# An attention stage on one core: where the query and key loads stand in SP's queue, and which queue carries the denominators

## The chip, the cores and the metric

The kernel runs on one core of a Trainium2 chip. The metric is the device time of one execution in microseconds (us). The engines are PE (TensorE), ACT (ScalarE), DVE (VectorE), POOL (GpSimd) and SP (SyncE, which here only issues DMAs); sixteen DMA engines move the data.

## The reference, cut to what matters

Eight batches of a 256 x 512 activation pass four layers: cross-attention, a ternary-weight feed-forward layer, a long convolution and an fp8 feed-forward layer. The change is in the first. Its attention is, with 16 heads of 16 rows each:

```python
q = einsum('oc,bct->bot', Wq, target) + bq      # 256 rows: 16 heads x 16
k = einsum('oc,bcs->bos', Wk, source) + bk
dot = einsum('bhdt,bhds->bhts', q, k) / sqrt(16)
dot = mask * dot - (1 - mask) * 1e6
amap = softmax(dot, axis=-1) * mask
x = x + tanh(g) * einsum('bhts,bhds->bhdt', amap, v)
```

## The kernel before, in words

Each layer is a phase, a block in which all engines run their own instruction lists and meet only in semaphores; the next phase begins when all engines have ended theirs. The projection phase writes the queries and keys to DRAM, split into three bf16 parts (`q_parts`, `k_parts`), as rows of 512 values (1 KB) ordered by head and then by row within the head.

The attention phase works in 16 **units**, u = 2b + h: batch b and half h of the heads (8 heads). A unit's operands are stacked in `Q` and `K`, four slots each: six blocks of 16 partitions hold products of bf16 parts, 8 further rows (partitions 96 to 103) hold mask and running maximum. `load_unit` (lines 505 to 516) fills a slot with 14 DMAs: 12 of 128 KB (16 partitions by 8 heads by 1 KB) and two of 64 KB for the mask.

Per unit, PE computes every head's scores twice. For unit u+1 (second half) and u+2 (first half) it makes the score tiles `ps_m` (L707), of which DVE takes the row maxima (L793, 32 per unit). They are turned, ACT copies them out as `mrow` (L653), and SP places them in the unit's slot (`place_max`, L529). For unit u itself PE makes the transposed scores `ps_s` (L728), ACT takes the exponential (L675), and PE multiplies by the values (L738). One extra column of the values gives the sums of the exponentials, the denominators. ACT evacuates the result in two halves, `num` and `odd_heads` (L664).

The **denominators' round trip** of a unit runs in the next unit: `gather_den` writes their rows to DRAM with two DMAs (L544, L545), waits for them, reads them back spread over 128 partitions (L547) and copies the odd heads' results beside the even ones with four DMAs (L550); DVE inverts them (L807); `store_inv` writes the inverse to DRAM (L556) and `spread_inv`, after a wait for that, reads it back broadcast to all rows (L562, 256 KB). POOL then normalises: three multiplications and additions of 128x512 (L623, L627, L631), the last into `X`. DVE takes the layer-norm statistics of unit u-2 from `X` in the third of the eight steps of unit u (L54).

POOL also makes ternary weights for the next layer in every unit (`weights`, L637 and L641, three of each, after ACT's rounding L687), from a 768 KB load `w_sweep` (L524). In every second unit it multiplies the mask by the gate (L612), and SP loads the next batch's values and mask (`load_batch`).

SP issues all DMAs from one list, in the order of the code. In unit u this is: the load of unit u+2 (after the scores of unit u-2), `gather_den` of unit u-1 with its two waits, every second time `load_batch`, `store_inv`, `place_max` of unit u+1, `spread_inv`, `load_weights` of unit u+1. PE waits for the load of unit u+2 in the middle of unit u.

Of the kernel before, what the change touches and what calls it, by code (L numbers as in the profile page):

```python
# [11 lines left out]
P = 128  # L12
B = 8
C = 256
L = 512
CT = C // P
LT = L // P
ROWT = B * CT
HEADS, HD = 16, 16
UH = 8  # L20
# [408 lines left out]
def phase_attention(core, ctx, A):  # L429
# [7 lines left out]
    DW = UH * L // P  # L437
    with ExitStack() as free:
# [14 lines left out]
        odd = sb("odd_heads", [P, 2, L], F32)  # L453
        den = sb("den", [P, 2, DW], F32)
# [38 lines left out]
        def over_batches(eng, batch):  # L493

            batch(0, 0, True, False)
            with eng.Fori(0, (B - 2) // 2) as i:
                batch(2 * i + 1, 1, False, False)
                batch(2 * i + 2, 0, False, False)
            batch(B - 1, 1, False, True)

        with nc.Block() as block:

            @block.sync
            def _(sp):
                def load_unit(b, slot, h, fresh=False):
                    for blk in range(BLOCKS):
                        for dst, src, part in ((Q, core.q_parts, Q_PART[blk]), (K, core.k_parts, K_PART[blk])):
                            s = src[bass.ds(b, 1), part, h * P:(h + 1) * P, :]
                            sp.dma_start(dst[blk * HD:(blk + 1) * HD, slot],
                                         s.rearrange("a (h d) l -> d (a h) l", d=HD)).then_inc(qk_loaded[slot], 16)  # L510
                    if fresh:
                        sp.wait_ge(zeroed[slot], 2)
                    for dst, src in ((Q, core.mask_q), (K, core.mask_k)):
                        s = src[bass.ds(b, 1)].rearrange("a r l -> r a l").to_broadcast([EXTRA, UH, L])
                        sp.dma_start(dst[MASK_ROW:MASK_ROW + EXTRA, slot], s).then_inc(qk_loaded[slot], 16)

                def load_batch(b, par):
                    sp.dma_start(V[:, par].rearrange("p a h d -> p (a h d)"),
                                 core.v_rows[bass.ds(b, 1)].rearrange("a p n -> p (a n)")).then_inc(v_loaded[par], 16)
                    sp.dma_start(mb[:, par, :], A["mask"][bass.ds(b, 1), 0, :].to_broadcast([P, L]))\  # L520
                        .then_inc(v_loaded[par], 16)

                def load_weights(u, h):
                    sp.dma_start(wc[:, h], A["w3"][bass.ds(u, 1)].rearrange("a p m l -> p (a m) l"))\  # L524
                        .then_inc(wc_loaded[h], 16)

                def place_max(v, slot, h):
                    sp.wait_ge(mrow_ready, v + 1)
                    sp.dma_start(Q[MAX_ROW:MAX_ROW + 2, slot], mrow[:]).then_inc(m_placed[h], 16)  # L529

                load_unit(0, 0, 0, fresh=True)
                load_unit(0, 1, 1, fresh=True)
                load_batch(0, 0)
                load_weights(0, 0)
                load_weights(1, 1)
                sp.wait_ge(zeroed[2], 2)
                sp.wait_ge(zeroed[3], 2)
                place_max(0, 0, 0)

                def gather_den(u, h, b):  # L540

                    sp.wait_ge(u_ready, 2 * u + 2)
                    rows = core.den_rows[h].rearrange("(g two) l -> two g l", two=2)
                    sp.dma_start(rows[0], num[HD:P:32, h, :]).then_inc(den_out[h], 16)  # L544
                    sp.dma_start(rows[1], odd[HD:P:32, h, :]).then_inc(den_out[h], 16)  # L545
                    sp.wait_ge(den_out[h], 32 * (b + 1))
                    sp.dma_start(den[:, h, :], core.den_rows[h].rearrange("q (s n) -> (q s) n", n=DW))\  # L547
                        .then_inc(den_placed[h], 16)
                    for g in range(4):
                        sp.dma_start(num[32 * g + HD:32 * g + 32, h, :], odd[32 * g:32 * g + HD, h, :])\  # L550
                            .then_inc(num_placed[h], 16)

                def store_inv(u, h):

                    sp.wait_ge(inv_ready, u + 1)
                    sp.dma_start(core.inv_rows[h].rearrange("q (s n) -> (q s) n", n=DW), inv[:, h, :])\  # L556
                        .then_inc(inv_out[h], 16)

                def spread_inv(h, b):

                    sp.wait_ge(inv_out[h], 16 * (b + 1))
                    sp.dma_start(inv_all[:, h, :], core.inv_rows[h].unsqueeze(1).to_broadcast([UH, HD, L]))\  # L562
                        .then_inc(all_placed[h], 16)

                def batch(b, par, first, last):
                    for h in range(2):
                        u = 2 * b + h
                        if not last:
                            if not first:
                                sp.wait_ge(scores_done, 2 * STEPS * (u - 1))  # L570
                            load_unit(b + 1, 2 * (1 - par) + h, h)
                        if not (first and h == 0):
                            gather_den(u - 1, 1 - h, b + h - 1)
                        if h == 1 and not last:
                            if not first:
                                sp.wait_ge(pv_step, 2 * STEPS * b)
                                sp.wait_ge(w_ready, 2 * b)
                            load_batch(b + 1, 1 - par)
                        if not (first and h == 0):
                            store_inv(u - 1, 1 - h)  # L580
                        if h == 0:
                            place_max(u + 1, 2 * par + 1, 1)
                        elif not last:
                            place_max(u + 1, 2 * (1 - par), 0)
                        if not (first and h == 0):
                            spread_inv(1 - h, b + h - 1)
                        if not (first and h == 0) and not (last and h):
                            sp.wait_ge(w_ternary, 3 * u)
                            load_weights(u + 1, 1 - h)
                    if last:  # L590
                        gather_den(u, h, b)
                        store_inv(u, h)
                        spread_inv(h, b)

                over_batches(sp, batch)

            @block.gpsimd
            def _(pool):
                for slot in (1, 3):
                    nc.gpsimd.memset(Q[96:P, slot], 0.0).then_inc(zeroed[slot], 1)  # L600
                    nc.gpsimd.memset(K[96:P, slot], 0.0).then_inc(zeroed[slot], 1)
# [3 lines left out]
                def batch(b, par, first, last):  # L605
                    for h in range(2):
                        u = 2 * b + h
                        if not (first and h == 0):
                            normalise(u - 1, 1 - h, 1 - par if h == 0 else par, b + h - 1)
                        if h == 0:  # L610
                            pool.wait_ge(v_loaded[par], batch_loads(b, par))
                            nc.gpsimd.tensor_tensor(mb[:, par, :], mb[:, par, :],  # L612
                                                    core.tanh_g[:, 0:1].to_broadcast([P, L]), ALU.mult)\
                                .then_inc(gate_ready, 1)
                            pool.wait_ge(gate_ready, b + 1)
                        weights(u, h)
                    if last:
                        normalise(u, h, par, b)

                def normalise(u, h, par, b):  # L620

                    pool.wait_ge(all_placed[h], 16 * (b + 1))
                    nc.gpsimd.tensor_tensor(inv_all[:, h, :], inv_all[:, h, :], mb[:, par, :], ALU.mult)\  # L623
                        .then_inc(w_ready, 1)
                    pool.wait_ge(w_ready, u + 1)
                    pool.wait_ge(num_placed[h], 64 * (b + 1))
                    nc.gpsimd.tensor_tensor(num[:, h, :], num[:, h, :], inv_all[:, h, :], ALU.mult)\  # L627
                        .then_inc(att_ready, 1)
                    pool.wait_ge(att_ready, u + 1)
                    xt = X[:, u:u + 1, :]  # L630
                    nc.gpsimd.tensor_tensor(xt, xt, num[:, h:h + 1, :], ALU.add).then_inc(x_updated, 1)  # L631
# [1197 lines left out]
```

## Time and profile before

| | |
|---|---|
| median of 3 runs | 1381.76 us (1378.74 to 1382.11) |
| the profiled execution | 1371.15 us, span of its instructions 1369.3 us |
| PE, DVE busy | 1113.3 us (81%), 1033.2 us (75%) |
| ACT, POOL busy | 668.1 us (49%), 523.4 us (38%) |
| row maxima L793, DVE | 512 instructions, 683 ns each, 322.2 us |
| exponentials L675, ACT | 256 instructions, 1022 ns each, 249.9 us |
| q_stack and k_stack loads | 96 each of 128 KB, from SP |

A row of the profile gives a group's busy time and, behind the bar, how long the engine had stood idle just before those instructions and who released it. The timeline gives, for each instruction or merged run of them, its start, duration, line and tiles. A DMA row's duration is the time that the issuing queue spent on it, not the transfer. All times in the rows are counted from the span's start.

### The profile page before, as it was taken

To read this page: it belongs to the slowest core of one execution; us is meant where nothing else is said; L and a number is where in the kernel's file an instruction comes from. 1 tells how busy PE (TensorE), PEld (TensorE's weight loads), DVE (VectorE), ACT (ScalarE), POOL (GpSimd) and SP (SyncE) were. 2 spreads that over 40 slices of the span, in tenths; PEclk is the share of its full clock that TensorE was granted. 3 is DMA by queue.
4 is the path that set the end of the run, shared out by engine and by line. 5 is a ranking of instruction groups with operands and counts; after the bars stand their busy time and mean duration, and the time that the engine had idled before them with its cause. 6 is when DMAs were issued, how large, how long until landed. Compare 5 with 4: busy or idle time off the path is not lost. (4 is left out here: it accounts for less than half of the span.)

```text
span 1369.3 us, 16346 instructions
## 1 busy us (share of the span) xinstructions
PE 1113.3 (81%) x4725; PEld 447.5 (33%) x4802; DVE 1033.2 (75%) x1587; ACT 668.1 (49%) x783; POOL 523.4 (38%) x384
## 2 busy tenths in 40 slices
PE   0887279998879987983799998599999999259777
PEld 0443112222222222220344444344444444134232
DVE  5765488887767877751799997388788887767898
ACT  0355308776657766684466665211000000386796
POOL 0466601244332442355011111477888787000021
PEclk9999659999989999997999999799999999579889
DMA  7398797677756776621311110111111111000011
GB/s 266 127 338 319 199 146 83 119 153 108 125 90 124 151 111 115 114 71 58 151 47 46 40 36 16 35 62 62 62 62 50 58 62 46 1 0 0 0 62 62
DMA packets 84274, 129.33 MB, mean 94 GB/s; under 512 B 13544, under 2 KB 53864, under 8 KB 83696
## 3 DMA queue, kind: packets, MB, share of 16 engines
q1 hardware_dynamic: 84224, 128.72, 38.8%
q8 instruction: 24, 0.39, 0.1%
q14 instruction: 26, 0.21, 0.1%
HBM read 104.44 MB, written 21.89 MB: 92 GB/s over the span
## 5 line engine op out<-in xcount | busy, mean ns | idle before, releaser
L793 DVE TENSOR_REDUCE mneg<-ps_m 128x1 f32<-128x512 f32 x512 | 322.2, 683 | 93.8 <-PE ps_m L707 78.3
L1337 PE MATMUL ps_y<-kv,toeplitz_sb 128*128 128x512 f32 x640 | 279.6, 596 | 8.7 <-POOL kv L1249 8.7
L675 ACT ACTIVATE probs<-ps_s 128x1024 f32<-128x1024 f32 x256 | 249.9, 1022 | 51.9 <-PE ps_s L728 51.9
L707 PE MATMUL ps_m<-k_stack,q_stack 128*128 128x512 bf16 x489 | 181.9, 410 | 55.3 <-DMA k_stack<-mask_k 50.4
L1337 PEld LDWEIGHTS ps_y<-kv,toeplitz_sb 128*128 128x128 f32 x640 | 121.1, 191 | 155.0 <-issue 155.0
L728 PE MATMUL ps_s<-q_stack,k_stack 128*128 128x512 bf16 x492 | 151.0, 387 | 21.1 <-ACT probs L675 11.2
L738 PE MATMUL ps_o<-probs,v_all 128*17 128x512 f32 x1024 | 140.1, 620 | 0.4 <-ACT probs L675 0.4
L1249 POOL TENSOR_TENSOR kv<-vT,ctxT_sb 128x2048 f32<-128x2048 f32 x32 | 118.7, 3711 | 40.0 <-PE ps_y L1337 32.6
L972 PE MATMUL ps_g<-w,xT_f 128*128 128x512 bf16 x491 | 116.7, 384 | 8.4 <-DVE h_f L1119 6.6
L623 POOL TENSOR_TENSOR inv_all<-inv_all,mb_b 128x512 f32<-128x512 f32 x16 | 20.4, 1274 | 254.9 <-DMA inv_all<-inv_rows 254.9
L707 PEld LDWEIGHTS ps_m<-k_stack,q_stack 128*128 128x128 bf16 x512 | 42.2, 99 | 219.4 <-DVE mneg L793 104.5
L1403 DVE TENSOR_TENSOR z<-ps_y,ctxT_sb 128x1024 f32<-128x1024 f32 x64 | 77.9, 1218 | 47.3 <-PE ps_y L1337 47.3
L1302 ACT ACTIVATE w_anchor<-w_f 128x512 f32<-128x512 f32 x32 | 20.1, 628 | 180.6 <-DMA w_f<-in_w 180.6
L1154 POOL TENSOR_TENSOR X<-X,down_sums 128x512 f32 (+1 forms) x16 | 20.5, 1283 | 195.6 <-ACT down_sums L1015 195.6
L1660 PE MATMUL ps_fp<-w 128*128 128x512 bf16 x251 | 67.7, 423 | 21.5 <-DVE w L1727 10.9
L1411 DVE TENSOR_REDUCE vT<-z 128x256 f32<-128x2304 f32 x32 | 81.7, 2553 | 1.1
L54 DVE BATCH_NORM_STATS2 bn<-X (+1 forms) x64 | 42.3, 682 | 42.8 <-POOL X L631 21.2
L728 PEld LDWEIGHTS ps_s<-q_stack,k_stack 128*128 128x128 bf16 x512 | 45.8, 98 | 81.0 <-ACT probs L675 33.9
L641 POOL TENSOR_SCALAR w<-w_sweep 128x512 bf16<-128x512 f32 x48 | 70.4, 1488 | 1.3
L1027 ACT ACTIVATE sg_f<-ps_g,sc_f 128x512 f32<-128x512 f32 x64 | 42.7, 686 | 57.0 <-PE ps_g L972 37.7
L972 PEld LDWEIGHTS ps_g<-w,xT_f 128*128 128x128 bf16 x512 | 48.4, 99 | 65.1 <-DVE h_f L1119 10.3
L326 PE MATMUL ps_a<-xn_a,w_qkv 128*128 128x512 f32 x64 | 30.6, 622 | 38.4 <-DVE xn_a L365 38.4
(163 smaller groups left out, 1662.6 us busy)
## 6 DMA issues: line engine op xcount, KB each, us to landing
w_sweep<-in_w SPq DMA_DIRECT2D x8, 1536.0 KB, 8.5
q_stack<-q_parts SPq DMA_DIRECT2D x96, 128.0 KB
k_stack<-k_parts SPq DMA_DIRECT2D x96, 128.0 KB
w_sweep<-in_w SPq DMA_DIRECT2D x16, 768.0 KB, 6.5
w_sweep<-in_w SPq DMA_DIRECT2D x16, 512.0 KB, 3.3
toeplitz_sb<-in_toeplitz SPq DMA_DIRECT2D x32, 256.0 KB, 2.6
w_f<-in_w SPq DMA_DIRECT2D x32, 256.0 KB, 2.9
q_parts<-qk_part SPq DMA_DIRECT2D x24, 256.0 KB, 4.0
```

The lines of the kernel that those rows point to most:

```text
L641: nc.gpsimd.tensor_scalar(core.w3[:, m].rearrange("p a b -> p (a b)")[:, u * L:(u + 1) * L], wc[:, h, m, :], MAGIC, None, ALU.subtract).th ...
L675: nc.scalar.activation(pr[:, k % 2, 2 * slot:2 * slot + 2, :], S[:, 2 * slot:2 * slot + 2, :], ACT.Exp).then_inc(exp_done, 1)
L707: nc.tensor.matmul(M[:, bank(j), :], Q[:, slot, hd, tc * P:(tc + 1) * P], K[:, slot, hd, :], start=True, stop=True).then_inc(max_mm, 1)
L728: mm = nc.tensor.matmul(S[:, g, :], K[:, slot4, hd, (k % LT) * P:(k % LT + 1) * P], Q[:, slot4, hd, :], start=True, stop=True)
L738: mm = nc.tensor.matmul(O[32 * g:32 * g + HD + 1, :], V[:, par, sc, h * UH + 2 * g + G, :], pr[:, k % 2, g, :], start=(sc == 0), stop=(sc ...
L793: nc.vector.tensor_reduce(mneg[:, h, tile % LT, tile // LT:tile // LT + 1], M[:, bank(j), :], AX.X, ALU.max, negate=True).then_inc(max_red, 1)
L972: mm = nc.tensor.matmul(G[:, c % 2, j, :], xT[:, par, k, :], wt[:, k, c * L:(c + 1) * L], start=(k == 0), stop=(k == LT - 1))
L1249: nc.gpsimd.tensor_tensor(kv[:, g % 2].rearrange("p l (b j i) -> p (l b) j i", b=B, j=GROUP), over_j(group(vT, g)), over_i(group(cT, g)), ...
L1337: mm = nc.tensor.matmul(Y[:, q % 3, l2, :], T[:, g % 2, (lt - m) * P:(lt - m + 1) * P], kv[:, g % 2, m, :], start=(m == 0), stop=(m == lt))
L1403: nc.vector.tensor_tensor(z[:, g % 2, NB // 2 * half:NB // 2 * (half + 1), :, 0:GROUP], Y[:, q % 3].rearrange("p l (b j i) -> p (l b) j i" ...
L1411: nc.vector.tensor_reduce(group(vT, g), z[:, g % 2], AX.X, ALU.add).then_inc(red_ready, 1)
L1660: mm = nc.tensor.matmul(D[:, r, :], h8[:, j % 4, L * t + r * P:L * t + (r + 1) * P], proj[:, ot, :], start=(i == 0 and t == 0), stop=(i == ...
```

## The change

- `load_unit` reads rows of `q_parts` and `k_parts` that are ordered by row within the head first, then by head, so that one partition's eight heads are 8 KB in a row. The projection weights and biases are permuted on the host (`by_dim`) so that the rows are produced in that order. Number and size of the DMAs stay.
- In SP's list the load of unit 2 stands before the first `place_max`, and in unit u the load of unit u+3 is the last entry, after `load_weights`, with a wait for the scores of unit u-1.
- `gather_den`, `store_inv` and `spread_inv` leave SP and are issued by POOL: `gather_den` of unit u-1 ahead of the gate and the ternary weights of unit u, the other two and the normalisation after them. Before, the normalisation stood ahead of the weights.
- SP's list is written out for all batches instead of looping.

```diff
-                                         s.rearrange("a (h d) l -> d (a h) l", d=HD)).then_inc(qk_loaded[slot], 16)
+                                         s.rearrange("a (d h) l -> d (a h) l", d=HD)).then_inc(qk_loaded[slot], 16)
...
                 load_weights(0, 0)
+                load_unit(1, 2, 0, fresh=True)
                 load_weights(1, 1)
-                sp.wait_ge(zeroed[2], 2)
-                sp.wait_ge(zeroed[3], 2)
                 place_max(0, 0, 0)
...
                     for h in range(2):
                         u = 2 * b + h
-                        if not last:
-                            if not first:
-                                sp.wait_ge(scores_done, 2 * STEPS * (u - 1))
-                            load_unit(b + 1, 2 * (1 - par) + h, h)
-                        if not (first and h == 0):
-                            gather_den(u - 1, 1 - h, b + h - 1)
                         if h == 1 and not last:
                             if not first:
                                 sp.wait_ge(pv_step, 2 * STEPS * b)
                                 sp.wait_ge(w_ready, 2 * b)
                             load_batch(b + 1, 1 - par)
-                        if not (first and h == 0):
-                            store_inv(u - 1, 1 - h)
                         if h == 0:
                             place_max(u + 1, 2 * par + 1, 1)
                         elif not last:
                             place_max(u + 1, 2 * (1 - par), 0)
-                        if not (first and h == 0):
-                            spread_inv(1 - h, b + h - 1)
                         if not (first and h == 0) and not (last and h):
                             sp.wait_ge(w_ternary, 3 * u)
                             load_weights(u + 1, 1 - h)
-                    if last:
-                        gather_den(u, h, b)
-                        store_inv(u, h)
-                        spread_inv(h, b)
-
-                over_batches(sp, batch)
+                        if u + 3 < 2 * B:
+                            if u:
+                                sp.wait_ge(scores_done, 2 * STEPS * u)
+                            load_unit((u + 3) // 2, (u + 3) % 4, (u + 3) % 2, fresh=u == 0)
+                for b in range(B):
+                    batch(b, b % 2, b == 0, b == B - 1)
...
             def _(pool):
+                def gather_den(u, h, b):
+                    pool.wait_ge(u_ready, 2 * u + 2)
+                    rows = core.den_rows[h].rearrange("(g two) l -> two g l", two=2)
+                    pool.dma_start(rows[0], num[HD:P:32, h, :]).then_inc(den_out[h], 16)
+                    pool.dma_start(rows[1], odd[HD:P:32, h, :]).then_inc(den_out[h], 16)
+                    pool.wait_ge(den_out[h], 32 * (b + 1))
+                    pool.dma_start(den[:, h, :], core.den_rows[h].rearrange("q (s n) -> (q s) n", n=DW))\
+                        .then_inc(den_placed[h], 16)
+                    for g in range(4):
+                        pool.dma_start(num[32 * g + HD:32 * g + 32, h, :], odd[32 * g:32 * g + HD, h, :])\
+                            .then_inc(num_placed[h], 16)
+                def store_inv(u, h):
+                    pool.wait_ge(inv_ready, u + 1)
+                    pool.dma_start(core.inv_rows[h].rearrange("q (s n) -> (q s) n", n=DW), inv[:, h, :])\
+                        .then_inc(inv_out[h], 16)
+                def spread_inv(h, b):
+                    pool.wait_ge(inv_out[h], 16 * (b + 1))
+                    pool.dma_start(inv_all[:, h, :], core.inv_rows[h].unsqueeze(1).to_broadcast([UH, HD, L]))\
+                        .then_inc(all_placed[h], 16)
...
                         if not (first and h == 0):
-                            normalise(u - 1, 1 - h, 1 - par if h == 0 else par, b + h - 1)
+                            gather_den(u - 1, 1 - h, b + h - 1)
...
                         weights(u, h)
+                        if not (first and h == 0):
+                            store_inv(u - 1, 1 - h)
+                            spread_inv(1 - h, b + h - 1)
+                            normalise(u - 1, 1 - h, 1 - par if h == 0 else par, b + h - 1)
                     if last:
+                        gather_den(u, h, b)
+                        store_inv(u, h)
+                        spread_inv(h, b)
                         normalise(u, h, par, b)
...
+    def by_dim(v):
+        return np.ascontiguousarray(v.reshape(v.shape[:-1] + (CT, P // HD, HD)).swapaxes(-1, -2).reshape(v.shape))
```

## Rows read from the trace of the kernel before

**Rows 1.** Windows: busy PE, PEld, DVE, ACT, POOL; granted clock, DMA share, GB/s.

```profile
205.00:646.00 441.00, 372.54 (x2019) 102.16 (x2058) 312.30 (x529) 304.27 (x351) 167.77 (x151) 0.95 0.62 108
```

**Rows 2.** Waits between 160 and 650 us: total us, times, longest.

```profile
POOL inv_all L623 <- DMA inv_all<-inv_rows: 254.9, 16, 28.8
...
PE ps_m L707 <- DMA k_stack<-mask_k: 50.4, 11, 22.2
```

**Rows 3.** Timeline of ACT: start, us, line, tiles, count, idle and releaser.

```profile
220.98 0.57 ACT L653 ACTIVATE mrow<-ps_m 16x512 bf16<-16x512 bf16 x1
...
244.89 0.57 ACT L653 ACTIVATE mrow<-ps_m 16x512 bf16<-16x512 bf16 x1
...
254.42 0.60 ACT L664 ACTIVATE odd_heads<-ps_o 128x512 f32<-128x512 f32 x1 [0.85 <-PE ps_o L738]
...
326.54 0.57 ACT L653 ACTIVATE mrow<-ps_m 16x512 bf16<-16x512 bf16 x1
...
603.13 0.57 ACT L653 ACTIVATE mrow<-ps_m 16x512 bf16<-16x512 bf16 x1
```

**Rows 4.** Timeline of DVE: the statistics of the second unit.

```profile
262.18 0.68 DVE L54 BATCH_NORM_STATS2 bn<-X  x1
```

**Rows 5.** Timeline of SP's queue: one unit, from mrow to mrow.

```profile
296.45 0.70 SPq L529 DMA_DIRECT2D q_stack<-mrow  x1
...
300.07 0.67 SPq L562 DMA_DIRECT2D inv_all<-inv_rows  x1
...
301.65 0.33 SPq L509 DMA_DIRECT2D q_stack<-q_parts  x1
...
309.27 0.50 SPq L545 DMA_DIRECT2D den_rows<-odd_heads  x1
...
320.06 0.36 SPq L547 DMA_DIRECT2D den<-den_rows  x1
...
327.13 0.70 SPq L529 DMA_DIRECT2D q_stack<-mrow  x1
```

**Rows 6.** Timeline of PE: the stall of that unit.

```profile
319.82 0.60 PE L707 MATMUL ps_m<-k_stack,q_stack 128*128 128x512 bf16 x1 [4.41 <-DMA k_stack<-mask_k]
```

**Rows 7.** Windows: unit loads, weight sweep, stores of the stage before; columns as above.

```profile
183.00:184.00 1.00, 1.00 (x2) 0.15 (x2) 1.00 (x2) 0.00 (x0) 0.00 (x0) 0.50 1.11 114
...
193.00:194.00 1.00, 1.00 (x3) 0.20 (x2) 1.00 (x3) 0.00 (x0) 0.18 (x1) 0.50 1.00 414
...
154.00:156.00 2.00, 0.17 (x1) 0.09 (x1) 0.51 (x3) 0.00 (x0) 0.00 (x0) 0.50 1.03 343
```

**Rows 8.** Timeline of SP's queue with empty DMA queues, at the end.

```profile
633.14 2.44 SPq L550 DMA_DIRECT2D num<-odd_heads  x4
...
635.63 0.58 SPq L556 DMA_DIRECT2D inv_rows<-inv  x1
...
637.31 0.64 SPq L562 DMA_DIRECT2D inv_all<-inv_rows  x1
```

**Rows 9.** Timeline of POOL at the end of the stage.

```profile
612.22 1.04 POOL L612 TENSOR_TENSOR mb_b<-mb_b,tanh_g 128x512 f32<-128x512 f32 x1
...
613.35 2.00 POOL L637 TENSOR_SCALAR w_sweep<-w_sweep 128x512 f32<-128x512 f32 x3
...
615.43 4.40 POOL L641 TENSOR_SCALAR w<-w_sweep 128x512 bf16<-128x512 f32 x3
...
641.11 1.26 POOL L623 TENSOR_TENSOR inv_all<-inv_all,mb_b 128x512 f32<-128x512 f32 x1 [7.32 <-DMA inv_all<-inv_rows]
...
643.79 1.26 POOL L631 TENSOR_TENSOR X<-X,num 128x512 f32<-128x512 f32 x1
```

**Rows 10.** Timeline of PE: its first work and its first scores.

```profile
176.38 1.60 PE L707 MATMUL ps_m<-k_stack,q_stack 128*128 128x512 bf16 x3 [22.20 <-DMA k_stack<-mask_k]
...
204.75 0.59 PE L728 MATMUL ps_s<-q_stack,k_stack 128*128 128x512 bf16 x2
```

**Rows 11.** Timeline of SP's queue: the first placement of the maxima.

```profile
199.14 0.81 SPq L529 DMA_DIRECT2D q_stack<-mrow  x1
```

More of the change, by code:

```diff
@@ L534, in _ @@
                 load_weights(0, 0)
+                load_unit(1, 2, 0, fresh=True)
                 load_weights(1, 1)
-                sp.wait_ge(zeroed[2], 2)
-                sp.wait_ge(zeroed[3], 2)
                 place_max(0, 0, 0)
[L540 to L563, printed above, removed]
                 def batch(b, par, first, last):
@@ L1810 @@
         "x": arr("x"), "ctx": arr("ctx_2048"), "mask": arr("mask_Bx1x2048_fk1"), "g_xattn": arr("g_xattn"),
-        "g_ffn": arr("g_ffn"), "bq": columns(inputs["L0_xattn_bq"]), "bk": columns(inputs["L0_xattn_bk"]),
+        "g_ffn": arr("g_ffn"), "bq": columns(by_dim(inputs["L0_xattn_bq"])), "bk": columns(by_dim(inputs["L0_xattn_bk"])),
         "mask_cols": np.ascontiguousarray(inputs["mask_Bx1x2048_fk1"].reshape(B, LT, P).transpose(2, 0, 1)),
         "bv": arr("L0_xattn_bv"),
-        "wqT": np.ascontiguousarray(inputs["L0_xattn_Wq"].T), "wkT": np.ascontiguousarray(inputs["L0_xattn_Wk"].T),
+        "wqT": by_dim(inputs["L0_xattn_Wq"].T), "wkT": by_dim(inputs["L0_xattn_Wk"].T),
         "wvT": np.ascontiguousarray(inputs["L0_xattn_Wv"].T),
```

## The prediction

> **What bounds the kernel now.** Of the views I read the one by stretch first: the attention stage is 441 us of the 1369 us span, and only its code changes. In it DVE is busy 312 us, PE 373, ACT 304, POOL 168, and the DMA engines 0.62 of the time [rows 1]. No engine is full, so what matters is what each unit waits for. The timeline of ACT gives the length of a unit, as `mrow` (L653) comes once in each. From the second to the third it is 23.9 us. From the second to the sixteenth it is 603.13 - 220.98 = 382.1 us in 14 units, 27.3 us each [rows 3]. The 23.9 us are the floor that PE and DVE allow when nothing is late; 14 x 3.4 = 48 us of the stage are waits above it.
>
> The view of waits names them: PE waits 50.4 us for the loads of Q and K [rows 2]. (POOL's 254.9 us in the same view cost nothing as long as no one waits for POOL.) The timeline of SP's queue shows why the load is late. After `mrow` SP places it at 296.45, but issues `spread_inv` only at 300.07 and the unit's load from 301.65 on; the two `den_rows` DMAs, issued behind that load at 308.7 and 309.27, have landed only when the next entry goes out at 320.06, 10.8 us later, since they queue behind 1.7 MB [rows 5]. PE starts the first tile on this load at 319.82, after 4.41 us of waiting [rows 6], 18.2 us after the load's first issue. Next `mrow`: 30.7 us after the last one [rows 5].
>
> **The change, part by part.**
>
> *Position of the loads.* "Three units ahead" is a new index, not a new place. Before, the load of unit u+3 is the first entry of SP's unit u+1; now it is the last of unit u, with the same wait for the scores of unit u-1. In both cases `place_max` of unit u+1 and `load_weights` stand directly ahead. What is gone from between is `spread_inv`: between 0.9 us (its issue and a gap) and the 3.6 us of the unit above [rows 5]. The load then starts about 2 us after `mrow`, and its 18.2 us fit the unit to within some tenths. I put a unit that waits for nothing else at 24.2 us, against the floor of 23.9: that would save 14 x 3.1 = 43 us.
>
> *The longer pieces.* Eight rows of 1 KB become one of 8 KB. What that is worth depends on what holds the loads at 114 GB/s with the DMA engines full, where the 6 KB pieces of `w_sweep` go at 414 [rows 7]. It is not the 1 KB piece by itself: the stores of the projection stage, also in 1 KB pieces but over 128 partitions, go at 343 [rows 7]. A load writes only 16 partitions, before and after. So I take it as unchanged, 1.2 us per 128 KB; the other end of the bound is 343 to 414 GB/s, 5 us per unit instead of 16. The Trainium skill, SBUF — State Buffer, "Door 1: The DMA port swizzle", gives the reason: 16 neighbouring partitions reach 4 of 16 ports, which by the page's 435 GB/s is 109 GB/s. By that rule the trace agrees, and nothing is gained from longer pieces.
>
> *The start.* PE begins at 176.38 on the first load and reaches the first scores at 204.75 [rows 10], soon after `place_max` of unit 0 is issued at 199.14 into an empty queue [rows 11]. Now the load of unit 2 and a sweep stand ahead of it. The sweeps end at about 197 (414 GB/s until 194 [rows 7]); without the second of them the load of unit 2 begins at 195. 12 x 1.2 + 2.4 (two masks of 8 partitions, reckoned at half that rate) = 17 us, and 2 for the sweep: the placement lands at 216 instead of before 204.75. **+11 us** at the unchanged rate; 0 if loads ran at 343.
>
> *The round trip on POOL.* Off SP, `den_rows` no longer queue behind the load. But POOL waits for each landing itself, in line with its own work. The engine had 168 of 441 us of work [rows 1]; now everything between is serial. From rows with empty DMA queues, per unit: first `den_rows` issue 0.6 and the trip of the second 1.7 (`inv_rows` at 635.63 had landed by 637.31); `den` and four `num` 0.35 + 2.44 = 2.8; half of a gate 0.5; weights 613.35 to 619.83, 6.5; `inv_rows` 1.7; `inv_all` 637.31 to 641.11, 3.8; normalising 641.11 to 645.05, 3.9 [rows 8, 9]. Sum **21.5 us**. Two prices are missing.
>
> First, POOL's own issue of a DMA, which this trace doesn't show. Bounds: 0 more than on SP, whose nine cost 5.0 us [rows 5, 8], and 1 us each, +4 (POOL's shortest instruction, a clip, takes 0.67 [rows 9]). I take 0.25 each, +2.3. The Trainium skill, DMA: Bandwidth & Descriptors, "Latency and other measured facts", has 1 us to the first byte on this path against 0.6 on SP's; three trips would add 1.2 us, inside these bounds.
>
> Second, sharing the DMA engines with the load, which is in flight 18 us of each unit, from 4 us after `mrow`. That is when `inv_rows` and `inv_all` go. In SP's single queue `inv_all` went ahead of the load; now both run at once. An engine's 8 KB share of one 128 KB DMA takes 1.2 us, so each turn taken with a load costs 1.2. Least: 0. Most: the 10.8 us of `den_rows` behind a whole load [rows 5]. `inv_rows` is one turn, 1.2; `inv_all` has 256 KB of 2 KB pieces, at least a few turns: I take 2.5, 3.0 us. Sum +4.2; it is nearer the low end, as turns are taken, not a whole load waited out. The skill page's "Queues, rings and completion order" says that an engine goes round its queues packet by packet; no row here shows two data queues at once.
>
> POOL's cycle: 21.5 + 2.3 + 4.2 = **28.0 us**, above 24.2. So POOL is the bound. It makes the others late as soon as it lags 7.2 us: DVE's statistics of unit u-2 run 7.2 us after `odd_heads` is evacuated (255.02 to 262.18 [rows 3, 4]), they wait for POOL's last addition, and behind them on DVE stand the maxima for which PE waits.
>
> *The sum*, along POOL. Its first gather starts at 231 + 11 = 242. 12 cycles with a load in flight, 12 x 28.0 = 336; 3 without (units 13 to 15), 3 x 23.8 = 71; last round trip without weights 21.5 - 6.5 - 0.5 + 2.3 = 17. End 666, against 645.05 before [rows 9]: **+21 us**. 1371.15 + 21 = 1392 for the profiled execution; that lies 10.6 us below the median of the runs, which gives 1403. The weights' move ahead of the normalisation costs nothing more: ACT's rounding is done before POOL, being late, arrives. SP's written-out list issues the same DMAs; I cost it at nothing, since SP waits for `mrow` anyway.
>
> **The rivals.**
>
> *POOL keeps up* (the other side). If POOL's cycle is at most 24.2 us, sharing and issue costing under 2.7 us together, units run at 24.2: 43 saved, less 11 at the start, and about 6 at the end, where units 14 and 15 are shorter than POOL's cycle. -26: 1356. For it: it needs only quick turns, and the weights can overlap ACT. Against: three trips that POOL waits out and 11 us of arithmetic in 24 us leave no slack, and any lag pushes the next trips into the next load. The decisive point is 24.2; the break-even with before is lower in rate, 26.2 us per cycle, (645 - 242 - 71 - 17)/12.
>
> *The longer pieces do speed the loads.* Then they take 5 us, nothing is contended, the start is 11 us earlier (17.4 us from issue to first tile becomes 7) and no +11. -35 -11 = -46: 1336. For it: no row shows 1 KB pieces loaded into 128 partitions. Against: the stores at 343.
>
> *Gain and loss cancel*: sharing at 2.4 us per unit, 1378 to 1386.
>
> *The turns are dearer*: 4 us more per cycle is 12 x 4 = 48: 1451.
>
> **Numbers.** POOL the bound and slower 0.47, cancelling 0.08, POOL keeps up 0.31, faster loads 0.14. Within 0.3% (4 us) of before a measurement can't tell it from no change. Faster 0.45, same 0.08, slower 0.47. The likeliest is 1403; its own range is 1387 to 1451. Since cases of both signs hold much, the range reaches down to the faster loads: 1336 to 1450.
>
> **What would show it.** Right: `mrow` to `mrow` 27 to 29 us and steady; POOL without idle time except on landings; DVE's statistics waiting for POOL's addition; PE waiting for DVE, no longer for loads; `inv_all` taking over 6 us from issue to L623; first scores at about 216. Wrong: units of 24 us; unit loads above 200 GB/s; POOL's DMAs landing in 2 us beside a load; first scores at 205.

## The result, and the profile after

The changed kernel takes 1479.68 us (median of 4 runs, 1478.55 to 1481.6) against 1381.22 us before. The ratio is 1.0717, interval 1.0699 to 1.0736. The profiled execution takes 1478.55 us, its span is 1476.8 us, against 1371.15 us before. The change costs 107 us there.

The attention stage first, by the view of stretches, with the columns of [rows 1]:

```profile
205.00:750.00 545.00, 391.52 (x2060) 106.44 (x2060) 312.09 (x527) 304.16 (x351) 246.01 (x295) 0.85 0.51 88
```

545 us in place of 441 [rows 1], with the same work on DVE (312) and ACT (304). POOL has 78 us more, its own DMA issues. The DMA engines are less busy than before (0.51 against 0.62), so the stage lacks neither work done nor bandwidth: it waits. The view of waits of the attention stage (total, times, longest) says for what:

```profile
PEld ps_m L703 <- DVE mneg L789: 206.0, 160, 10.3
ACT probs L671 <- PE ps_s L724: 177.0, 96, 19.5
DVE bn L54 <- POOL X L627: 127.1, 14, 15.4
POOL inv_all L585 <- DMA inv_rows<-inv: 117.3, 16, 11.8
POOL inv_all L619 <- DMA inv_all<-inv_rows: 104.0, 16, 9.6
POOL den L570 <- DMA den_rows<-odd_heads: 29.5, 15, 9.9
```

It is read from the bottom up. POOL waits 117.3 + 104.0 us for the two trips of the inverses; DVE's statistics wait 127.1 us for POOL's last addition, 14 times; PE waits for DVE's maxima and ACT for PE. PE's wait for unit loads [rows 2] is gone but for the first one. One whole cycle of POOL, nearly the same in every unit but the first, by its timeline (start, duration, line, tiles, and in brackets the idle time ahead and who ended it):

```profile
492.43 0.60 POOL L567 DMA_DIRECT2D den_rows<-num  x1
493.04 0.57 POOL L568 DMA_DIRECT2D den_rows<-odd_heads  x1
494.99 0.58 POOL L570 DMA_DIRECT2D den<-den_rows  x1 [1.39 <-DMA den_rows<-odd_heads]
495.56 1.95 POOL L573 DMA_DIRECT2D num<-odd_heads  x4
497.52 1.05 POOL L601 TENSOR_TENSOR mb_b<-mb_b,tanh_g 128x512 f32<-128x512 f32 x1
498.67 2.00 POOL L633 TENSOR_SCALAR w_sweep<-w_sweep 128x512 f32<-128x512 f32 x3
500.75 4.40 POOL L637 TENSOR_SCALAR w<-w_sweep 128x512 bf16<-128x512 f32 x3
505.11 0.65 POOL L579 DMA_DIRECT2D inv_rows<-inv  x1
515.56 0.64 POOL L585 DMA_DIRECT2D inv_all<-inv_rows  x1 [9.81 <-DMA inv_rows<-inv]
523.76 1.26 POOL L619 TENSOR_TENSOR inv_all<-inv_all,mb_b 128x512 f32<-128x512 f32 x1 [7.56 <-DMA inv_all<-inv_rows]
...
526.44 1.26 POOL L627 TENSOR_TENSOR X<-X,num 128x512 f32<-128x512 f32 x1
527.65 0.60 POOL L567 DMA_DIRECT2D den_rows<-num  x1
```

The cycle is 35.2 us. Half of it, 18.65 us, lies between the issue of `inv_rows` at 505.11 and the first multiplication at 523.76, where the same two trips take 637.31 - 635.63 and 641.11 - 637.31, 5.5 us, on empty queues [rows 8, 9]. The other trip, `den_rows`, is awaited at 493 to 495, when no load is in flight: 1.95 us. On DVE and in SP's queue, same unit:

```profile
527.88 0.69 DVE L54 BATCH_NORM_STATS2 bn<-X  x1 [9.05 <-POOL X L627]
```

```profile
501.92 0.64 SPq L529 DMA_DIRECT2D q_stack<-mrow  x1
502.61 0.41 SPq L524 DMA_DIRECT2D w_sweep<-in_w  x1
503.07 0.43 SPq L509 DMA_DIRECT2D q_stack<-q_parts  x1
...
509.00 0.31 SPq L515 DMA_DIRECT2D k_stack<-mask_k  x1
```

The load begins at 503.07, two microseconds ahead of `inv_rows`, and at 18 us for a load [rows 5, 6] it has landed at about 521; by stretches of one microsecond the bytes stop at 522. The first trip runs within it and has landed 6 us before that, at 515.56; the second ends with it. The sweep of 768 KB issued at 502.61 is in flight too, until about 507.

### The profile page after: what moved, and what is told of

It is laid out like the page before. It is cut to its first block and busy times, and to the rows that moved or that the text cites. A ratio compares the mean times of both kernels' runs of the same rounds, so it can differ in the third digit from the quotient of the medians.

```text
span 1476.8 us, 16091 instructions
## 1 busy us (share of the span) xinstructions
PE 1131.9 (77%) x4802; PEld 449.3 (30%) x4802; DVE 1033.9 (70%) x1587; ACT 668.0 (45%) x783; POOL 601.8 (41%) x528
## 5 line engine op out<-in xcount | busy, mean ns | idle before, releaser
L703 PE MATMUL ps_m<-k_stack,q_stack 128*128 128x512 bf16 x512 | 196.0, 420 | 125.6 <-DVE mneg L789 103.2
L724 PE MATMUL ps_s<-q_stack,k_stack 128*128 128x512 bf16 x512 | 164.6, 407 | 25.3 <-DMA q_stack<-mrow 13.9
L54 DVE BATCH_NORM_STATS2 bn<-X (+1 forms) x64 | 42.4, 684 | 148.7 <-POOL X L627 127.1
L968 PE MATMUL ps_g<-w,xT_f 128*128 128x512 bf16 x512 | 120.0, 383 | 7.1 <-DVE h_f L1115 6.3
L1656 PE MATMUL ps_fp<-w 128*128 128x512 bf16 x256 | 66.6, 414 | 22.5 <-DVE w L1723 12.3
L619 POOL TENSOR_TENSOR inv_all<-inv_all,mb_b 128x512 f32<-128x512 f32 x16 | 20.2, 1263 | 104.0 <-DMA inv_all<-inv_rows 104.0
L955 PE MATMUL ps_d<-w,hT_f 128*128 128x512 bf16 x256 | 59.5, 387 | 1.6 <-ACT hT_f L996 1.6
```

Of the source, the lines that this page charges most:

```text
L703: nc.tensor.matmul(M[:, bank(j), :], Q[:, slot, hd, tc * P:(tc + 1) * P], K[:, slot, hd, :], start=True, stop=True).then_inc(max_mm, 1)
L724: mm = nc.tensor.matmul(S[:, g, :], K[:, slot4, hd, (k % LT) * P:(k % LT + 1) * P], Q[:, slot4, hd, :], start=True, stop=True)
L968: mm = nc.tensor.matmul(G[:, c % 2, j, :], xT[:, par, k, :], wt[:, k, c * L:(c + 1) * L], start=(k == 0), stop=(k == LT - 1))
L1656: mm = nc.tensor.matmul(D[:, r, :], h8[:, j % 4, L * t + r * P:L * t + (r + 1) * P], proj[:, ot, :], start=(i == 0 and t == 0), stop=(i == ...
```

## The experiments

The theory after the first profile: the two trips of the inverses are slow only because a load is in flight that is bound by the ports through which it writes its few neighbouring partitions, and POOL adds them up in line with its own work. Rivals: the 8 KB pieces make each turn at a DMA engine long; DMAs from POOL are slow in themselves; the gathering and its waits on POOL are what costs; the loss lies in the start.

**Piece size.** `after_1k`: the changed kernel with the layout of before, pieces of 1 KB.

```diff
-   s.rearrange("a (d h) l -> d (a h) l", d=HD)).then_inc(qk_loaded[slot], 16)
+   s.rearrange("a (h d) l -> d (a h) l", d=HD)).then_inc(qk_loaded[slot], 16)
```

> The changed kernel with the 1 KB pieces of before (rows ordered by head again); everything else as changed. Theory of the pieces: each of POOL's small pieces waits for one piece of the unit load on its DMA engine, 1.2 us at 8 KB and 0.15 at 1 KB. Then the trip of inv_rows falls from about 9.8 us to about 3, inv_all from 8.2 to under 5, POOL's cycle from 34 to about 25 us, and the time to about 1370 us. Theory of the ports: POOL's pieces wait for the full write ports, whatever the piece; trips and time stay, about 1479 us.

Measured: 1473.9 us, ratio 1.0715 (1.0669 to 1.076). The same two trips in it:

```profile
502.83 0.65 POOL L579 DMA_DIRECT2D inv_rows<-inv  x1
512.48 0.63 POOL L585 DMA_DIRECT2D inv_all<-inv_rows  x1 [9.00 <-DMA inv_rows<-inv]
520.49 1.26 POOL L619 TENSOR_TENSOR inv_all<-inv_all,mb_b 128x512 f32<-128x512 f32 x1 [7.37 <-DMA inv_all<-inv_rows]
```

9.65 and 8.0 us, against 10.45 and 8.2. Pieces an eighth as long shorten the trips by 0.8 and 0.2 us at most, where the theory of the pieces asked for 3 and under 5 us: that rival falls. The prediction priced a turn by a DMA's 8 KB share of an engine; that share is the same in both layouts, so this run does not test that price. The 10.45 us of the trip themselves refute it.

`before_8k`: the kernel before, with the 8 KB pieces alone.

> The kernel before with the 8 KB pieces alone. If the four write ports that 16 partitions reach hold the load, nothing moves: loads at about 110 GB/s, 1381 us within 5. If the piece's length held it, a load would take under 8 us instead of 16, and the time would fall to about 1335 us.

Measured: 1381.5 us, ratio 1.003 (1.001 to 1.005). First tile on a load at 179.09 us, in place of 176.38 [rows 10]. The longer piece gives nothing, by the interval it is a hair slower.

**The ports.** `before_spread`: the kernel before, each block of 16 rows in every sixth partition of 96 instead of 16 neighbours. `Q` and `K` are permuted alike, so the sums over partitions are the same.

```diff
-   sp.dma_start(dst[blk * HD:(blk + 1) * HD, slot],
+   sp.dma_start(dst[blk:BLOCKS * HD:BLOCKS, slot],
```

> The kernel before, same DMAs, bytes and 1 KB pieces; only the 16 partitions of a block are taken in steps of 6 (blk, blk+6, ... blk+90) instead of side by side. Theory of the ports: the load goes at over 200 GB/s and takes under 9 us instead of 16, PE's waits for loads go, units fall to 24 us and the first tile starts 7 us earlier: 1320 to 1335 us. If the pieces or the source hold the load: 1381 us.

Measured: **1318.12 us, ratio 0.9581 (0.9548 to 0.9614)**. One microsecond within a load, by stretch (columns as in [rows 1]), and `mrow` of two units:

```profile
393.00:394.00 1.00, 1.00 (x9) 0.13 (x8) 1.00 (x2) 0.36 (x1) 1.00 (x1) 1.00 1.11 211
```

```profile
456.32 0.57 ACT L653 ACTIVATE mrow<-ps_m 16x512 bf16<-16x512 bf16 x1
480.21 0.57 ACT L653 ACTIVATE mrow<-ps_m 16x512 bf16<-16x512 bf16 x1
```

The DMA engines are as full as before, but move 211 GB/s instead of 114 [rows 7]. Every unit from the second on now takes 23.9 us: the floor that the prediction read from [rows 3], and no wait for loads is left but for the first one.

`before_spread_8k` adds the 8 KB pieces to it.

> The kernel before with the spread partitions and the 8 KB pieces together. In the run with 1 KB pieces the load went at about 205 GB/s and the units at 23.9 us, their floor. If the pieces now hold the load, the first tile starts up to 3 us earlier and the time falls to 1314; if the ports still hold it (13 of 16 reached, three twice), 1318 as with 1 KB.

Measured: 1319.1 us, ratio 0.9612 (0.9585 to 0.9638). Piece length is worth nothing at this rate either. But at this rate something else comes near: SP needs longer to issue a load that is spread. Its queue and the mean of 8 us within the first load of `before_spread`:

```profile
163.02 0.60 SPq L509 DMA_DIRECT2D q_stack<-q_parts  x1
163.66 0.60 SPq L509 DMA_DIRECT2D k_stack<-k_parts  x1
```

```profile
162.00:170.00 8.00, 0.00 (x0) 0.00 (x0) 6.33 (x5) 0.00 (x0) 8.00 (x3) 0.50 0.64 201
```

One DMA of 128 KB goes out every 0.64 us (0.47 in the kernel before), which is 205 GB/s; the load runs at 201, with the DMA engines busy for only 0.64 of the time. The first load of the spread kernels is thus held by SP's issuing, and says nothing of what the ports or longer pieces could give beyond that. In the later units a sweep ahead of the load builds up a backlog, and there the 211 GB/s stand at full engines.

`before_step2` interleaves only pairs of blocks, each in every second partition of 32.

```diff
-   sp.dma_start(dst[blk * HD:(blk + 1) * HD, slot],
+   sp.dma_start(dst[blk // 2 * 32 + blk % 2:(blk // 2 + 1) * 32:2, slot],
```

> The kernel before with blocks 2k and 2k+1 interleaved, each block in every second partition of 32, instead of every sixth of 96. Theory of the partition range (what counts is over how wide a range of partitions one DMA writes): 32 neighbouring partitions give twice the 110 GB/s of 16, so 0.6 us per 128 KB, a load of 8 us, units of 23.9 us and a time like that of steps of six, ratio 0.957 to 0.962. Rival (what helps is only a range of near 96 partitions, or that two DMAs behind each other write into different places): 110 to 160 GB/s, loads of 11 to 16 us, ratio 0.965 to 1.00.

Measured: 1317.82 us, ratio 0.9559 (0.9479 to 0.964; only 2 runs, hence the wide interval). Within a load:

```profile
393.00:394.00 1.00, 1.00 (x7) 0.31 (x4) 0.67 (x2) 0.51 (x2) 0.92 (x2) 1.00 1.11 202
```

Sixteen partitions spread over a range of 32 are enough for about 205 GB/s, nearly twice the rate of 16 neighbours. The Trainium skill, SBUF — State Buffer, "Door 1: The DMA port swizzle", has it so: 32 neighbouring partitions reach 8 of 16 ports, 16 reach 4. By that rule the traces agree in the ratio, at 202 to 211 and 114 GB/s; the 109 GB/s for 16 partitions that the prediction took from the page is exceeded here, by the 114, and over 14 us of the first loads of the kernel before by a mean of 122.

**The start.** `after_first`: the changed kernel with `place_max(0, 0, 0)` and the second sweep back ahead of the load of unit 2.

```diff
-                load_unit(1, 2, 0, fresh=True)
                 load_weights(1, 1)
                 place_max(0, 0, 0)
+                load_unit(1, 2, 0, fresh=True)
```

> The changed kernel with the first placement of the maxima and the second weight sweep issued ahead of the load of unit 2. Theory: the first scores start at about 205 us instead of 218, and the time falls by 13 us to 1466. If the load of unit 2 is then late for the middle of unit 0, less than that: 1475.

Measured: 1463.94 us, ratio 1.0642 (1.058 to 1.0704), 2 runs that lie 10 us apart. First scores at 206.79 in place of 217.92, and by the two traces the stage's last statistics on DVE run 9.7 us earlier. `before_first` is the mirror: the kernel before with this start alone.

```diff
+                load_unit(1, 2, 0, fresh=True)
                 load_weights(1, 1)
...
+                            if not (first and h == 0):
                                 load_unit(b + 1, 2 * (1 - par) + h, h)
```

> The kernel before with the start of the change alone: the load of unit 2 stands ahead of the second sweep and of the first placement, all else as before. My theory (position only, as in the prediction, and as the 13 to 15 us of the run with the placement put back ahead): first scores at 217 to 218 instead of 205, everything behind it shifted, 11 to 13 us slower: about 1385 here against 1372 to 1376, ratio 1.008 to 1.010. Rival (the unit load that is out of the way early is won back in units 1 and 2, which then wait for no load): ratio 1.000 to 1.003.

Measured: 1389.01 us, ratio 1.0079 (1.0041 to 1.0116), 11.1 us above the kernel before as it ran beside it (1377.91). First scores:

```profile
219.90 1.03 PE L730 MATMUL ps_s<-q_stack,k_stack 128*128 128x512 bf16 x2 [13.37 <-DMA q_stack<-mrow]
```

The start costs 11 us alone and about 10 within the change.

**What stretches the trips.** `after_spread`: the changed kernel with steps of six, so that a load is in flight half as long.

> The changed kernel, only with each block's 16 partitions taken in steps of 6, as in the run of the kernel before with that edit. If POOL's trips are slow because the loads keep four write ports full (theory of the ports), the loads end after 8 us, inv_rows and inv_all fall from 9.8 and 8.2 us to about 3 and 5, POOL's cycle from 34 to 24 or 26 us, the first scores start at about 205: 1325 to 1355 us. If the trips are slow because any second queue beside a load is served late, they stay near 9 and 8 us until the load ends, which is at half the time: about 1400.

Measured: 1375.02 us, ratio 1.0019 (0.9998 to 1.0039), above what was expected. POOL's rows:

```profile
424.00 0.60 POOL L567 DMA_DIRECT2D den_rows<-num  x1
...
436.66 0.65 POOL L579 DMA_DIRECT2D inv_rows<-inv  x1
442.52 0.63 POOL L585 DMA_DIRECT2D inv_all<-inv_rows  x1 [5.21 <-DMA inv_rows<-inv]
447.16 1.27 POOL L619 TENSOR_TENSOR inv_all<-inv_all,mb_b 128x512 f32<-128x512 f32 x1 [4.00 <-DMA inv_all<-inv_rows]
...
451.06 0.60 POOL L567 DMA_DIRECT2D den_rows<-num  x1
```

The trips take 5.9 and 4.6 us, about half of before, yet the cycle is 27.1 us: 16.6 of POOL's work, issues and first trip (to 436.66, and from 447.16 on) and 10.5 of the inverses' trips. That is over the 23.9 us that the others need, so POOL stays the bound. My expectation had put the two trips at 3 and 5 us, 8 together, and the time at 1325 to 1355 us; its rival, trips near 9 and 8 us and about 1400, is missed too. So this run shows that a shorter load shortens the trips, not that the ports as such are what holds them.

`after_few_bytes`: from unit 4 on each load carries one of the eight heads (the other operands stay those of earlier units, so this part of the computation is not that of the reference). The number of DMAs and their places are the same.

```diff
+                    hs = UH if fresh else 1
-   sp.dma_start(dst[blk * HD:(blk + 1) * HD, slot],
-                s.rearrange("a (d h) l -> d (a h) l", d=HD)).then_inc(qk_loaded[slot], 16)
+   sp.dma_start(dst[blk * HD:(blk + 1) * HD, slot, 0:hs],
+                s.rearrange("a (d h) l -> d (a h) l", d=HD)[:, 0:hs]).then_inc(qk_loaded[slot], 16)
```

> The changed kernel, but from unit 4 on the loads of Q and K carry one head of eight (16 KB instead of 128 KB in each of the 12 DMAs); the rest of the slot keeps older data. Number of DMAs, semaphores and order stay. Every theory that blames the load's bytes in flight: inv_rows about 2 us, inv_all about 4, POOL's cycle 22 to 24.5 us, ended by the units of 24 us, 1340 to 1355 us with the 13 us of the start still lost. If POOL's issuing or its order is the cause: cycle stays at 34 us, 1470.

Measured: 1356.65 us, ratio 0.9886 (0.9854 to 0.9918).

```profile
437.29 0.65 POOL L580 DMA_DIRECT2D inv_rows<-inv  x1
440.24 0.63 POOL L586 DMA_DIRECT2D inv_all<-inv_rows  x1 [2.31 <-DMA inv_rows<-inv]
444.70 1.27 POOL L620 TENSOR_TENSOR inv_all<-inv_all,mb_b 128x512 f32<-128x512 f32 x1 [3.83 <-DMA inv_all<-inv_rows]
```

Trips of 3.0 and 4.5 us, a cycle of 24 us, and units of 23.9. With the bytes gone and all DMAs and waits still there, the loss is gone: it is the load in flight, not POOL's issuing, that stretches the trips. The changed kernel's own last units, which have no load to make, say the same. First `inv_rows` and `inv_all` beside a sweep alone, then with nothing beside them:

```profile
675.59 0.64 POOL L579 DMA_DIRECT2D inv_rows<-inv  x1
678.58 0.64 POOL L585 DMA_DIRECT2D inv_all<-inv_rows  x1 [2.36 <-DMA inv_rows<-inv]
...
739.10 0.57 POOL L579 DMA_DIRECT2D inv_rows<-inv  x1
741.11 0.63 POOL L585 DMA_DIRECT2D inv_all<-inv_rows  x1 [1.43 <-DMA inv_rows<-inv]
```

`inv_rows` takes 2.0 us alone, so DMAs from POOL are not slow in themselves, and 3.0 beside the sweep, the same as here: about 1 us of the stretched trip is the sweep's, which the prediction left out, and some 7.5 us the load's.

**Whose trip is it?** `after_act_store`: the changed kernel with `store_inv` issued from ACT's queue after `mrow`, so that the trip begins without POOL. The line removed is one of POOL's list, the ones added are ACT's.

```diff
-                            store_inv(u - 1, 1 - h)
...
+                    act.wait_ge(inv_ready, u + 1)
+                    act.dma_start(core.inv_rows[h].rearrange("q (s n) -> (q s) n", n=DW), inv[:, h, :])\
+                        .then_inc(inv_out[h], 16)
```

> The changed kernel, but inv_rows is issued from ACT's queue, after the copy of mrow, instead of from POOL's. It then goes out 2 us ahead of the load instead of some us behind its start. Theory: the trip is slow only because the load is in flight; ahead of it it takes 2 us from any queue, POOL's cycle falls by about 8 us to 26, about 1385 us. If it still takes over 6 us, then a second hardware queue is served late as well, behind the load issued after it.

Measured: 1449.77 us, ratio 1.0564 (1.053 to 1.060), far above what was expected.

```profile
424.93 0.72 POOL L579 DMA_DIRECT2D inv_all<-inv_rows  x1
440.90 1.26 POOL L611 TENSOR_TENSOR inv_all<-inv_all,mb_b 128x512 f32<-128x512 f32 x1 [15.25 <-DMA inv_all<-inv_rows]
```

The store is issued at 420.30, two microseconds ahead of the load (422.47), and POOL has no wait for it; but `inv_all` alone takes 16.0 us instead of 8.2. The wait has moved from one trip to the other; of 18.65 us only 2.7 are saved.

`after_half`: the start put right, and both DMAs of the inverses back in SP's list ahead of the unit's load. Only the gathering, the weights and the normalisation stay on POOL. The lines added are SP's, the ones removed POOL's.

```diff
+                        if u:
+                            store_inv(u - 1, 1 - h)
                         if h == 0:
                             place_max(u + 1, 2 * par + 1, 1)
                         elif not last:
                             place_max(u + 1, 2 * (1 - par), 0)
+                        if u:
+                            spread_inv(1 - h, b + h - 1)
...
-                            store_inv(u - 1, 1 - h)
-                            spread_inv(1 - h, b + h - 1)
```

> The changed kernel with the first placement back ahead of the load of unit 2, and with the inverses' two DMAs back in SP's list ahead of the unit's load (the store ahead of the placement, the broadcast behind it); the gathering, its waits, the ternary weights and the normalisation stay on POOL in the changed kernel's order. My theory (the loss is the inverses' two trips beside the load in flight, 17 to 18 us where they take 5 alone): POOL's cycle falls from 34 to at most 20 us of work and waits of its own, POOL is no longer the bound, units of 24 to 25 us, 1335 to 1350, ratio 0.97 to 0.985. Rival (what costs is the gathering and its waits on POOL, which delay the weights and the additions): still above 1400, ratio over 1.02.

Measured: 1384.02 us, ratio 1.0024 (0.998 to 1.0068), some 40 us above what was expected, and below the rival's 1400. Against `after_first` it wins 80 us, and the inverses' trips are quick. But look at POOL and SP:

```profile
402.71 0.67 POOL L585 DMA_DIRECT2D den_rows<-num  x1 [1.18 <-ACT odd_heads L662]
403.37 0.57 POOL L586 DMA_DIRECT2D den_rows<-odd_heads  x1
415.63 0.57 POOL L588 DMA_DIRECT2D den<-den_rows  x1 [11.68 <-DMA den_rows<-odd_heads]
```

```profile
394.83 0.42 SPq L509 DMA_DIRECT2D q_stack<-q_parts  x1
...
420.25 0.33 SPq L542 DMA_DIRECT2D inv_rows<-inv  x1
421.26 0.66 SPq L529 DMA_DIRECT2D q_stack<-mrow  x1
...
423.15 0.43 SPq L509 DMA_DIRECT2D q_stack<-q_parts  x1
```

POOL, now earlier, gathers beside the load, and `den_rows` takes 12.3 us (403.37 to 415.63) where it took 1.95. Its landing closes a ring: load (394.83), end of the load and of `den_rows` (415), `den`, inversion, the store in SP's list (420.25), and only then the next load (423.15), 28.3 us later. PE waits for that load again.

`after_half_spread` is `after_half` with steps of six.

> The same kernel with each block in every sixth partition of 96. If the rate of the loads and the place of the inverses are the only two things that count, both are now cured and the units are at PE's and DVE's floor of 23.9 us: ratio 0.955 to 0.960, as the kernel before with steps of six (0.958). If the order of the change is worth something beyond (the load after the placement, gathering off SP), it comes out below 0.954; if POOL's waits still cost, above 0.963.

Measured: 1330.13 us, ratio 0.9649 (0.9586 to 0.9713). Its last `mrow` is at 553.9 against 551.1 in `before_spread`, so its units are nearly at the floor, and `den_rows` takes 5.5 to 8.3 us. The time over `before_spread` is mostly not in the units but behind them (last section). Nothing of the change's order beats the order of before once the loads are spread: the three kernels before with spread loads, 1317.8 to 1319.1 us and not to be told apart, are the fastest of the study.

## Why the prediction was wrong

The direction, to which the prediction gave 0.47 against 0.45 for faster, and the bound (POOL, with its trips in line) were right. The time was not: 1403 us was 77 us too low, outside the range to 1450, because the cost of a trip beside a load was put at a third of what it is.

*Floor and waits: right.* `before_spread` shows both: all its units take 23.9 us, and its attention stage ends at 592.95 in place of 645.05, 52.1 us earlier, of which 48 are the waits that the prediction counted and 3 the first load (first tile at 173.15 for 176.38).

*Position of the loads: not tested.* PE waits for no unit load but the first, but in a kernel where POOL is late for every unit that says little. What the position is worth, 24.2 us per unit, no run shows: where POOL's lag is gone at the full length of a load, in `after_half`, the load is late again by the ring above.

*Longer pieces: right.* Nothing (`before_8k`, `after_1k`, `before_spread_8k`), and the reason, over how narrow a range of partitions a load writes, is shown by two kernels that alter only this.

*The start: right.* First scores at 217.92 for 216; 11.1 us alone, for 11.

*POOL as the bound, through DVE's statistics: right.* 14 of these wait, 127.1 us, and PE waits for DVE.

*POOL's own issue cost: over-estimated.* Nine DMAs take 0.60 + 0.57 + 0.58 + 1.95 + 0.65 + 0.64 = 5.0 us, just what SP's nine cost, so 2.3 us too much. The trip of `den_rows` came out at 1.95 us for the 1.7 taken.

*Sharing with the load: the step that failed.* I priced a trip beside a load by turns of 1.2 us, 4.2 us in all. Measured in the unit shown: `inv_rows` 10.45 - 1.7 = 8.8 instead of 1.2, `inv_all` 8.2 - 3.8 = 4.4 instead of 3.0. The cycle is 28.0 + 7.6 + 1.4 - 2.3 = 34.7 us, and half a gate more in a unit that has one, which is the 35.2 measured. Together that is 13.2 us for the 4.2 taken, more even than the upper bound that I had named, the 10.8 us of `den_rows` behind a whole load [rows 5], which I dismissed because those stood in the same queue. The runs show that another queue is no shelter: `inv_rows`, `inv_all` or `den_rows`, whichever goes first beside the load, waits for most of what is left of it (10.45, 16.0 and 12.3 us). The Trainium skill, DMA: Bandwidth & Descriptors, "Back-pressure in remote DMA", says of transfers between cores that a saturated port clogs the path back and that "Stalled writes stall the source SDMA engine's other queues too." The three traces agree with this for loads from DRAM on one core, though none shows the engines' inner queues. Whether full ports hold the trips, or any bytes in flight ahead of them, stays open: each run that eased the ports also shortened the load, and the sweep, which writes 128 partitions, held `inv_rows` for 1 us of its own 2. The turn by turn rule that the prediction drew on gives 1.2 us and is not what was measured.

*The sum*, term by term. The first gather came at 245.84 for 242: +3.8. Twelve cycles with a load end at 663.99, 418.2 us for 336: +82.2, of which the first alone, 40.6 us, is 6 over the rest (there `den_rows` too meets a load and takes 10.4 us, then `inv_rows` meets the next and takes 12.5). Three without: 70.0 for 71. The last trip ends at 748.65 after 14.6 for 17. Together 3.8 + 82.2 - 1.0 - 2.4 = 82.6, which is 748.65 - 666. The phases behind took 3.9 us more than before, where I had nothing. That makes 86.5 us between the profiled execution and the 1392 predicted for it. Between the medians it is 77 because the kernel before had been profiled in an execution 10.6 us under its median, the changed kernel 1.1 under. Nearly all of the miss is the one term, twelve times over: 12 x 9.0 = 108 us by the unit shown, of which the over-estimated issue, 12 x 2.3, happened to take 28 back. The rival of dearer turns had the right sign and place, 4 us per cycle where it was 6.7.

## What to carry to other kernels

Before moving a round trip to another queue, ask what will be in flight in the DMA engines at that moment: here a small transfer beside a load into few partitions took 8 to 16 us instead of 2 to 4, from POOL's queue as much as in SP's, and the engine that waited for it in line with its own work paid the whole of it, each cycle. First look at what bounds the load: here the target rows spread over 32 or 96 partitions instead of 16, one index in one line, doubled the rate and gained 4.2%, more than any order of the queues. And a stretched trip that was cured handed its wait to the next one in the chain, in both kernels that tried it, so cost every trip beside the load, not the first.

## What the runs showed of the hardware

- DMAs of 128 KB into 16 neighbouring partitions ran at a mean of 122 GB/s in pieces of 1 KB (`before`, 162 to 176 us) and of 116 in pieces of 8 KB (`before_8k`, 164 to 178 us); into 16 partitions spread over 32 or 96 they ran at 202 to 211. SP took 0.64 us to issue one that was spread, 0.47 otherwise.
- The end of the phase was longer in every kernel in which POOL issued DMAs. The wait of DVE between its last statistics and the next phase, in the kernel before, in the changed one and in `after_half_spread`:

```profile
646.10 0.19 DVE L75 TENSOR_TENSOR ln_tmp<-bn 128x16 f32<-128x16 f32 x1 [0.32 <-PEq L501]
```

```profile
751.73 0.18 DVE L75 TENSOR_TENSOR ln_tmp<-bn 128x16 f32<-128x16 f32 x1 [2.35 <-PEq L501]
```

```profile
605.49 0.18 DVE L75 TENSOR_TENSOR ln_tmp<-bn 128x16 f32<-128x16 f32 x1 [8.80 <-PEq L501]
```

It is 0.32 us in the six kernels in which SP issues all DMAs of the stage, 2.35 in the five where SP and POOL split them as the change does, 8.80 in the two where SP has the inverses, and 10.11 where ACT issues the store. It does not depend on the rate of the loads. These 8.5 us are most of the 12 us between `after_half_spread` and `before_spread`. What the phase's end waits for there is not shown by any row and stays open.
- The granted clock of the stage was 0.95 before [rows 1], 0.85 after and 0.99 in `before_spread`; PE, which idles more the later POOL is, was busy 372.5, 391.5 and 355.0 us for the same work. In the changed kernel POOL sets the cycle, so by this reading the lower clock cost nothing more there.
